# A block of attention and experts: the last batch's way to its places, the tile table and the first rows moved

## The reference

```python
a = x + tanh(g_xattn) * cross_attention(layernorm(x), ctx)      # no projections
n = layernorm(a)
h = n + attention(rmsnorm(n, g1), wq, wk, wv, wo)               # rope, causal
xf = rmsnorm(h, g2)                                             # (4096, 256)
probs = softmax(xf @ w_router); topw, topi = top_k(probs, 2); topw /= sum(topw)
g = silu(einsum('td,xdh->txh', xf, wg)); u = einsum('td,xdh->txh', xf, wu)
y = h + einsum('txd,tx->td', einsum('txh,xhd->txd', g * u, wd), combine(topw, topi))
out = a + tanh(g_ffn) * y
```

## Time and profile before

| | |
|---|---|
| median of 3 runs | 1549.71 us (1542.04 to 1550.37) |
| profiled execution | 1551.29 us, its span 1549.5 us |
| granted clock of PE, mean | 0.980 |
| start to first scores on PE | 28.6 us |
| last scores of attention, ranks of batch 6 | until 1026.6 us |
| start of `up(0)` | 1030.9 us |
| start of `up(6)`, the first tile behind the early ones | 1095.8 us |

### The profile page before, as it was taken

How to read it: one execution, slowest core, us unless ns; L and a number is a source line. 1 busy time by engine, 2 the same in 40 slices (tenths; PEclk the granted TensorE clock), 3 DMA queues, 4 the chain that set the end, 5 groups by cost and what they waited for, 6 DMA issues and landing times.

```text
span 1549.5 us, 31596 instructions
## 1 busy us (share of the span) xinstructions
PE 1431.2 (92%) x9439; PEld 881.5 (57%) x9439; DVE 978.9 (63%) x2351; ACT 779.6 (50%) x1783; POOL 880.5 (57%) x1147
## 2 busy tenths in 40 slices
PE   3999999999999998999999998878899999999997
PEld 1332334444444444444444545557799999999996
DVE  5887757757766865865874755626555555555553
ACT  1576665665665674665556545543233333333332
POOL 7585776974977877787678777445321222222222
PEclk9899999999999999999999999999899999999999
DMA  7755465564575565556464545383353455255221
GB/s 199 193 161 175 110 193 162 171 208 129 167 210 158 181 177 173 170 170 202 120 209 138 162 153 172 135 301 99 62 153 101 92 149 152 42 153 152 38 43 11
DMA packets 116518, 230.20 MB, mean 149 GB/s; under 512 B 20101, under 2 KB 82949, under 8 KB 114310
## 3 DMA queue, kind: packets, MB, share of 16 engines
q1 hardware_dynamic: 81394, 150.29, 31.9%
q0 software_dynamic: 26032, 69.82, 16.3%
q10 hardware_dynamic: 8932, 8.07, 2.0%
HBM read 135.10 MB, written 93.14 MB: 147 GB/s over the span
## 4 chain that ended last, share of the span: by engine, by line
PE 71%; DVE 9%; POOL 7%; issue 5%; ACT 3%; DMA 2%; SPq 1%; another core or an unknown queue 1%; POOLq 0%; ACTq 0%; DVEq 0%
PE pv_ps L1113 10%; PE pv_ps L803 9%; PE max_ps L1075 9%; PE key_ps L1092 9%; PE key_ps L769 9%; PE max_ps L769 9%; DVE neg L1398 4%; PE aux L1161 4%; PE aux L1152 2%; PE aux L1145 2%; PE turn_ps L790 2%; ACT probs L1284 2%; PE key_ps L1095 1%; PE max_ps L1078 1%; PE turn_ps L1138 1%
## 5 line engine op out<-in xcount | busy, mean ns | idle before, releaser
L1398 DVE TENSOR_REDUCE neg<-max_ps 128x1 f32<-128x512 f32 (+3 forms) x864 | 542.3, 665 | 278.0 <-PE max_ps L1078 171.7
L1284 ACT ACTIVATE probs<-key_ps 128x512 f32<-128x512 f32 (+3 forms) x1024 | 499.6, 519 | 376.6 <-PE key_ps L1095 174.9
L1075 PE MATMUL max_ps<-k_stack,q_stack 96*128 96x512 bf16 (+3 forms) x1024 | 356.2, 351 | 32.2 <-DVE neg L1398 17.1
L1092 PE MATMUL key_ps<-q_stack,k_stack 99*128 99x512 bf16 (+3 forms) x1024 | 352.3, 345 | 26.3 <-ACT probs L1284 18.6
L612 POOL DMA_INDIRECT out<-part,whose x71 | 109.8, 1547 | 350.8 <-DVE part L660 275.8
L1075 PEld LDWEIGHTS max_ps<-k_stack,q_stack 96*128 96x128 bf16 x1024 | 101.2, 99 | 222.6 <-DVE neg L1398 122.5
L1092 PEld LDWEIGHTS key_ps<-q_stack,k_stack 99*128 99x128 bf16 x1024 | 100.8, 99 | 125.1 <-ACT probs L1284 61.2
L803 PE MATMUL pv_ps<-weights,hidden_t 128*128 (+1 forms) x1207 | 163.2, 289 | 1.4 <-DVE hidden_t L684 1.4
L769 PE MATMUL max_ps<-weights,rows_t 128*128 (+2 forms) x642 | 153.8, 385 | 0.0
L769 PE MATMUL key_ps<-weights,rows_t 128*128 (+2 forms) x636 | 152.2, 384 | 1.1 <-issue 1.1
L803 PEld LDWEIGHTS pv_ps<-weights,hidden_t 128*128 128x128 f32 x1207 | 150.3, 193 | 1.7 <-issue 1.7
(11 more groups left out here) (242 smaller groups left out, 2102.2 us busy)
## 6 DMA issues: line engine op xcount, KB each, us to landing
w_split<-w_parts POOLq DMA_DIRECT2D x32, 704.0 KB, 5.9
weights<-w_split SPq DMA_DIRECT2D x8, 2816.0 KB
weights<-w_split SPq DMA_DIRECT2D x8, 1280.0 KB
w_split<-w_parts POOLq DMA_DIRECT2D x16, 512.0 KB, 4.0
kept_sb<-kept SPq DMA_DIRECT2D x16, 512.0 KB
rows<-rows_in ACTq DMA_DIRECT2D x61, 129.0 KB
parts_cross_k<-parts_k SPq DMA_DIRECT2D x48, 128.0 KB
parts_cross_q<-parts_q SPq DMA_DIRECT2D x48, 128.0 KB
```

The costliest lines, as they stand in the source:

```text
L1075: r = mm(ps[:, 0:keys], q_stack[g][0:KROWS, hd, qt * P:(qt + 1) * P], k_stack[g][0:KROWS, hd, 0:keys], start=True, stop=not own)
L1092: r = mm(ps[:, q0:S], k_stack[g][0:KROWS + NEGROWS, hd, kt * P:(kt + 1) * P], q_stack[g][0:KROWS + NEGROWS, hd, q0:S], start=True, stop=no ...
L1284: act.activation(probs[:, kt % 2, hd, q0:S], key_ps[j % 2][:, q0:S], ACT.Exp).then_inc(m["exp_done"], 1)
L1398: v.tensor_reduce(neg[:, g % 2, hd - place_:hd + 1, qt], scores, op=ALU.max, axis=AX.X, negate=True).then_inc(m["max_red"], many)
```

## The change

1. The last batch's units move to tiles 0 to 2 (before: 0 to 3), and two new places for units exist: behind the first and behind the second chunk of `up`.
2. The table has one tile in each partition, so that an operation is `[128, 8]` and not `[1, 568]`; it has two parts in place of four, and links (waits between dependent operations) only where needed. One DMA on SP's queue, behind the eight paddings, brings its five columns into one partition. What waited for the table now waits for that DMA; ACT waits at tile 6 for table, scatters and paddings.
3. Batch 5's second scatter is in the stage of the first.
4. At the start POOL normalises batch 0 ahead of the ones of the key stacks, which are written as pairs, 1024 float32 in place of 2048 bf16 each.

```diff
+PAIR_OF_ONES = float(np.array([0x3F803F80], np.uint32).view(np.float32)[0])
+TABLE = 5
+EXPERT, OFFSET, ROW, OLD = 0, 1, 2, 3
-ATT_TURNS  LAST: in_tile(0, 0, 10)
+           LAST: in_tile(0, 0, 7)
-WO_HALVES  LAST: in_tile(1, 4, 6)
+           LAST: in_tile(0, 9, 11)
-H_SUMS     LAST: in_tile(1, 6, 8)
+           LAST: in_tile(0, 10, 13)
-H_SQUARES  LAST: in_tile(1, 6)
+           LAST: in_tile(0, 12)
-HN2_TURNS  LAST: in_tile(2, 4, 10)
+           LAST: in_tile(1, 11) + in_tile(2, 0)
-LOGITS     LAST: in_tile(3, 0)
+           LAST: in_tile(2, 7)
-CHOICES    LAST: in_tile(3, 1, 3, 5)
+           LAST: in_tile(2, 8, 9, 10)
-RANKS      LAST: in_tile(3, 10)
+           LAST: in_tile(2, 11)
-PLACES     LAST: in_tile(3, 11, 12, 13)
+           LAST: in_tile(2, 12, 13, 14)
-TABLE_PARTS = {0: in_tile(3, 14) + in_tile(4, 0, 10) + in_tile(5, 0)}
+TABLE_PARTS = {0: in_tile(3, 0) + in_tile(4, 0)}
-     LAST - 2: (stage(LAST - 1, 7), stage(LAST, 0)), LAST - 1: (stage(LAST, 3), stage(LAST, 5)), LAST: (stage(LAST, 7),) * 2}
+     LAST - 2: (stage(LAST - 1, 7),) * 2, LAST - 1: (stage(LAST, 3), stage(LAST, 5)), LAST: (stage(LAST, 7),) * 2}
...
-                AHEAD, TURNED, MADE, LED = (0, 4), (4, 10), (10, 13), (13, 16)
+                AHEAD, TURNED, CHUNK_0, CHUNK_1, MADE, LED = (0, 4), (4, 7), (7, 9), (9, 11), (11, 14), (14, 16)
+                BEGUN, ENDED = (0, 11), (11, 16)
...
                 def sync_rest(sp):
-                    sp.wait_ge(m["table"], 1)
+                    sp.wait_ge(m["table"], 16)
                     sp.wait_ge(m["scat"], B * 2 * QT * 16)
                     sp.wait_ge(m["pad"], 16 * E)
...
                         if EARLY <= j < TILES - ROW_RING:
+                            if j == EARLY:
+                                act.wait_ge(m["table"], 16)
+                                act.wait_ge(m["scat"], B * 2 * QT * 16)
+                                act.wait_ge(m["pad"], 16 * E)
...
                             r.then_inc(t_["up_mm"], 1)
+                            for u in tail_units(j, (CHUNK_0, CHUNK_1)[k]) if k < 2 else ():
+                                extra(u)
...
-                sp.dma_start(xn[0:1, :, :].rearrange("p t d -> p (t d)")[:, 0:TILES * E], c_table).then_inc(m["tab_ld"], 16)
...
                 end_rows(sp)
+                sp.wait_ge(m["tiles"], 1)
+                sp.dma_start(tiles_i[:, :, :].rearrange("p t c -> p (t c)"), tiles_p[0:TILES, :]).then_inc(m["table"], 16)
                 sync_rest(sp)
...
                     if part_ == 1:
-                        dve.wait_ge(m["tab_ld"], 16)
-                        link(v.tensor_tensor(passed, wide(cum, TILES), tile_no, ALU.is_le))
-                        link(v.tensor_reduce(expert_f, passed, op=ALU.add, axis=AX.X))
...
+                        v.tensor_scalar(skip, full_f, -float(P), None, ALU.mult)
+                        v.tensor_reduce(expert_f, passed, op=ALU.add, axis=AX.X)
+                        link(v.tensor_tensor(among, passed, full_f, ALU.mult))
...
+                        v.tensor_tensor(tiles_p[:, ROW:ROW + 1], row_f, begin[:, :], ALU.add).then_inc(m["tiles"], 1)
...
-                for g in range(G):
-                    g_.memset(k_stack[g][KROWS:KROWS + NEGROWS, :, :], 1.0).then_inc(m["ready_k"], 1)
-                    pool.wait_ge(m["ready_k"], g + 1)
...
                 values(0)
+                pool.wait_ge(m["v_cross"], 1)
+                for g in range(G):
+                    ones_row = k_stack[g][KROWS:KROWS + NEGROWS, :, :].rearrange("p h t -> p (h t)").bitcast(F32)
+                    g_.memset(ones_row, PAIR_OF_ONES).then_inc(m["ready_k"], 1)
+                    pool.wait_ge(m["ready_k"], g + 1)
                 x_rows(1)
```

More of the change, by code:

```diff
@@ L324, in one @@
             return sb(name, (1, *shape), dt)
-        expert_i, row_i, w_off = (one(n, TILES, dt=I32) for n in ("expert_i", "row_i", "w_off"))
-        old_i = [one(f"old_i{n}", TILES, dt=I32) for n in range(2)]
+        tiles_i = one("tiles_i", TILES, TABLE, dt=I32)
         cum_i, pad_i, order_i = (one(n, E, dt=I32) for n in ("cum_i", "pad_i", "order_i"))
         early_i = one("early_i", EARLY, dt=I32)
-        order, chosen, onward = one("order", E + 1), one("chosen", E, E), one("onward", E)
+        order, chosen, onward, begin = (sb(n, (P, *shape)) for n, shape in (("order", (E + 1,)), ("chosen", (E, E)), ("onward", (E,)), ("begin", (1,))))
+        tiles_p = sb("tiles_p", (P, TABLE), I32)
         padding = sb("padding", (P, DX))
@@ L424, in flamingo_block @@
                 h_sq h_rstd h_norm h_base gap_r gap_exp hot_r
-                rank_r route scat tab_ld pad_at pad first table hn2_twice""".split()
+                rank_r route scat pad_at pad first tiles table hn2_twice""".split()
             m = {n: sem("s_" + n, st) for n in names}
@@ L605, in add_up @@
                     if j >= EARLY:
-                        old = [pool.value_load(old_i[n][0:1, j:j + 1], min_val=16, max_val=added(TILES)) for n in range(2)]
+                        old = [pool.value_load(tiles_i[0:1, j, OLD + n:OLD + n + 1], min_val=16, max_val=added(TILES)) for n in range(2)]
                     pool.wait_ge(t_["y_done"], j + 2)
@@ L725, in tensor, with reg @@
                     mm, tr = nc.tensor.matmul, nc.tensor.transpose
-                    def reg(tab, j, most_):
-                        return pe.value_load(tab[0:1, j:j + 1], min_val=0, max_val=most_)
+                    def reg(column, j, most_):
+                        return pe.value_load(tiles_i[0:1, j, column:column + 1], min_val=0, max_val=most_)
                     def turn_rows(j):
@@ L1597, in _ @@
-                in_order, first_at = (turned["q"][0:1, 0, n * E:(n + 1) * E] for n in (6, 7))
-                full_i = full_i.bitcast(I32)
-                rest_of_line = turned["q"][0:1, 1, :]
-                expert_f, row_f, start_f, float_f = (rest_of_line[:, n * TILES:(n + 1) * TILES] for n in range(4))
-                int_a, int_b = (rest_of_line[:, n * TILES:(n + 1) * TILES].bitcast(I32) for n in (4, 5))
-                tile_no = by_expert(xn[0:1, :, :].rearrange("p t d -> p (t d)")[:, 0:TILES * E])
@@ new lines, in _ @@
+                in_order, full_f, cum, ones_e, passed, among, skip, end_f = (turned["q"][:, 0, n * E:(n + 1) * E] for n in range(8))
+                full_i = turned["q"][:, 0, 8 * E:9 * E].bitcast(I32)
+                expert_f, start_f, row_f, odd_f = (turned["q"][:, 0, 9 * E + n:9 * E + n + 1] for n in range(4))
+                halves_f = turned["q"][:, 0, 10 * E:10 * E + 2]
+                odd_i, halves_i = (turned["q"][:, 0, 11 * E + 2 * n:11 * E + 2 * n + w].bitcast(I32) for n, w in ((0, 1), (1, 2)))
@@ L1607, in table @@
+                counts_by = turned["q"][:, 1, 0:E * E].rearrange("p (t e) -> p t e", e=E)
                 def table(part_):
@@ L1639, in table @@
-                    if part_ == 3:
-                        link(v.tensor_tensor(among, wide(full_f, TILES), passed, ALU.mult))
-                        link(v.tensor_reduce(start_f, among, op=ALU.add, axis=AX.X))
-                        for n in range(2):
-                            link(v.tensor_scalar(int_a, start_f, float(1 - n), None, ALU.add))
-                            link(v.tensor_scalar(int_b, int_a, 1, None, ALU.logical_shift_right))
-                            link(v.tensor_copy(float_f, int_b))
-                            link(v.tensor_scalar(old_i[n][:, :], float_f, 16.0, 16.0, ALU.mult, ALU.add))
-                        v.tensor_scalar(cum_i[:, :], cum, 1.0, None, ALU.add).then_inc(m["table"], 1)
-                        dve.wait_ge(m["table"], 2)
+                        v.tensor_scalar(skip, full_f, -float(P), None, ALU.mult)
@@ new lines, in table @@
+                        v.tensor_reduce(expert_f, passed, op=ALU.add, axis=AX.X)
+                        link(v.tensor_tensor(among, passed, full_f, ALU.mult))
+                        v.tensor_tensor(skip, skip, onward[:, :], ALU.add)
+                        v.tensor_scalar(expert_f, expert_f, float(E - 1), None, ALU.min)
+                        link(v.tensor_reduce(start_f, among, op=ALU.add, axis=AX.X))
+                        v.tensor_copy(tiles_p[:, EXPERT:EXPERT + 1], expert_f)
+                        v.tensor_scalar(halves_i[:, 0:1], start_f, 1.0, None, ALU.add)
```

108 lines of the change are left out of this document (48 added, 60 removed).

## The result

The changed kernel takes 1554.69 us (median of 20 runs), the kernel before 1547.49 (20 runs): ratio 1.0042, 95% interval 1.0031 to 1.0054, so 6.5 us slower (4.8 to 8.4), where 3.4 us faster was forecast. That is above the forecast's own range, 1541 to 1551, and above the one that 8 cases in 10 were to lie in, 1537.5 to 1554. The profiled execution took 1555.01 us (span 1553.2).

What follows compares the result with a forecast made beforehand. PE, busy 1431.2 of 1549.5 us, was taken as the bound, so gains lay in its waits and low clock. Terms -3.9 + 5.9 + 1.1 - 8.2 + 1.7 = -3.4 us gave 1546.3, range 1541 to 1551 (8 in 10: 1537.5 to 1554).

Steps and rivals of the forecast that it cites:

- The start: Up to the first scores: POOL's first rows come 4.0 us earlier, gain 3.9 us, bounds 2 and 4.5.
- The scatter of batch 5: Step 7 of attention: PE waits for batch 6's rows, 5.9 us lost, plus 1.1 us for low clock.
- Tiles 0 to 6: Up to down(5): earlier places and rows of tile 6 gain 8.2 us, less 1.7 us for low clock.
- the arrival of PE at `turn_rows(6)`: Tile 6: PE arrives at 1081.3, rows come at 1085.4, leaving 4.1 us of waiting instead of 5.87.
- the ranks need no wait: Tile 2: two chunks of up, 2.4 us, cover DVE's choice, so PE does not wait for the ranks.
- 1.4 us of new waits between tiles 2 and 6: Eleven table operations on DVE, 2.4 us, ahead of hidden(3) push turn_hidden(3) and up(4) back by 1.4 us.
- the port rule: At the start: DVE and GpSimd share a port pair held per instruction; rows could wait 2 us, gain about 2.
- none at tile 6: Sign of being wrong: PE has no wait at turn_rows(6), where 2 to 5 us was expected.
- the DMA of the table: Behind SP's paddings, ahead of tile 6's row loads: costs nothing up to 1.5 us; 1.2 us was taken.
- my rivals: Scatter not stopping PE (0.17), faster paddings and last scatter (0.13), start giving nothing (0.12), slower stall at step 7 (0.13).
- the slower rival: End of attention: late first-half landing delays batch 6's rows 11 us, not 5.9; 1552.8 to 1557.3 us, chance 0.13.

Runs made afterwards that it cites:

- l_again_first: a_late_scatter with POOL's copy of the last batch's rows moved ahead of the first add-up; 0.9914 and, repeated, 0.9905 of the kernel before.
- session 3: Later round repeating earlier kernels beside the kernel before (1545.2 us); the changed kernel, unedited, took 0.9964 of it.
- sessions 1 and 4: Rounds measuring parts of the change apart, then again with a combined kernel; the kernel before took 1547.57 and 1548.95 us in them.
- a_late_scatter: Changed kernel with batch 5's second scatter put back behind the rows of batch 6; 0.9996 of the kernel before (1547.66 us), repeated 0.9936.

## Why the prediction was wrong

**The start** (-3.9 forecast): the mechanism is right, 3.28 us in the profile, 2.3 and 6.4 in the two measurements. The memsets took 4.56 us, not 3.8 (1.11 ns an element in f32, 0.92 in bf16 before); they ended at 22.14, ahead of the scores, so it cost nothing. The rows beside DVE took 1.2 us longer, of which 0.75 was left at their end (3.22 us earlier, for a start 3.97 earlier); that lies within the bounds of 0.1 to 1.

**The scatter of batch 5** (+5.9 and +1.1): the mechanism is right. PE waited 6.66 us against 5.9; the copy waited 1.77 for the landing, where I took 1.3. The clock was low for 6.4 us behind it, not for the 3 that I took. 7.1 us by the ratios with the standstill, 4.3 without, 10.2 alone; 7.0 forecast, so that the first of these meets it so closely is partly luck.

**Tiles 0 to 6** (-8.2, +1.7): wrong, +4.6 and +2.6 alone. The step that failed is the arrival of PE at `turn_rows(6)`: 1081.3 was forecast in the time of the kernel before; it was 1095.6 (1096.88 less the 1.26 by which `up(0)` began later), 14.3 us later. I had written that the ranks need no wait, and had priced 1.4 us of new waits between tiles 2 and 6, on DVE alone, and nothing on ACT. What the runs show in its place:

- ACT's standstill: 4.47 us of PE's waiting at `turn_rows(5)` and 1.7 of low clock behind. It also made the table's second part late, which then met POOL's base rows and took 5.0 us on DVE instead of 1.9 (ended by 1087.7): 2.56 us of waiting at `turn_hidden(4)`, then `up(5)` in about 6.3 us instead of 3.9.
- DVE behind POOL's instruction at the ranks: 1.80 us with 1.5 of low clock. I had kept the port rule for the start alone, and the table at 0.2 us an operation.

These are 14.4 us. The changed kernel without the standstill says how they divide: it passes `turn_rows(6)` at 1083.2 in the same time (1081.59, with `up(0)` 1.61 earlier than in the kernel before), after 0.79 us of waiting, where I had forecast an arrival at 1081.3 and the passage at 1085.4. So 12.4 us of the lateness come and go with the standstill, and the 3 us at the ranks stay; without the standstill the term was about right. The sign of being wrong that I had named and that came is "none at tile 6", no wait there.

The other half of that term was right. The places did come earlier, the rows of tile 6 no longer stop PE, the DMA of the table takes 3.1 us from its issue to the first row load (1087.74 to 1090.83; my upper bound was 2.55 + 0.5) and bounds nothing here. The 2.0 us that the prediction quotes beside it from the Trainium skill (DMA: Bandwidth & Descriptors, Anatomy of one DMA — SWDGE (gpsimd) path) is stated for DMAs that GpSimd issues, and this one is SP's; nothing hung on it. Where ACT does not stand still, the stretch of the tiles falls by 9.4 us (70.6 to 61.2), against 6.5 forecast with the clock and a bound of 16, and the kernel as a whole is 5.6 us faster than before.

The sum fits with the standstill, though loosely: start -2.3 to -6.4, scatter +7.1, tiles +2.6 to +4.6 gives +3.3 to +9.4; measured +6.5. None of my rivals was this one. The measured time lies in the slower rival's 1552.8 to 1557.3, by chance: it rested on a late landing in attention (from 5 us on), and the landing took 1.77. No case had an idle engine without a releaser move onto the path.

## What to carry to other kernels

- A stall that another stall hides is still in the trace. Before taking a wait off the path (5.87 us here), list the idle time of *every* engine in that stretch, also the idle time with an unknown releaser: that of ACT (6.75 us, 2.9 of them delay) stood right under it, and became the bound.
- Small DVE operations that stand beside POOL's long operations on 1024 elements (1.6 to 2.4 us) can cost as much as these; beside its scatters the table's first part kept to some 0.2 us an operation. Place them by POOL's timeline, or move POOL's work, as `l_again_first` does.
- When unlike edits all give the same large gain, measure an old kernel again beside them before believing any.

## What the runs showed of the hardware

- ACT, DVE and SP can all be slow to go on while POOL issues ten indirect DMAs in a row and SP eight DMAs (ACT idle for 6.0 to 10.8 us); the same ten and eight run without it in the changed kernel of session 3. On SP a register move then takes up to 704 ns for 29; the paddings take 13.8 to 14.0 us for 8.1 to 8.9 in the kernels with the new table, and 11.1 to 12.6 for 8.2 with the old. With it were all profiles of sessions 1 and 4 and the two first ones, without it all of 2, 3 and 5; sessions 1 and 3 were on one chip, 2 and 4 on another. Its cause isn't shown. `a_late_scatter` moved the same packets and bytes over its whole span with it and without it (150.29 and 69.82 MB on its two large queues), so more traffic of the kernel's own is not the cause.
- The Trainium skill (NOTIFIC — the notification-queue block, Interfaces) states that the block which takes an engine's records can press back on it and stall it. That would fit the slow steps, but no run here can show it, nor whether the standstill would be there in an execution that is not traced.
- The price of one and the same edit differs with the condition: the changed kernel is 1.0042 or 0.9964 of the kernel before, each with an interval of 0.0026 or less.
